# Expert rows on four 64x64 tiles with a folding product, and block attention's small products in four column groups

## What is computed

```python
x = x + attn(layernorm(x))                   # a: heads of 16 features, softmax over features
x = x + mlstm(layernorm(x), ctx, ctx)        # b: gated linear attention on the context
x = x + experts(layernorm(x))                # c: product-key experts + gated MLP
x = x + causal_attention(layernorm(x))       # d
x = x + block_attention(layernorm(x), ctx, mask)  # e: queries pooled over blocks of 16 tokens
x = x + local_layers(x)                      # 6 x (rotary windowed attention, GELU MLP)
```

```python
# c: 4 heads x 8 experts of 4096 for each token, rows of 256 features
scores, indices = top_k of the pairwise sums of two key scores
w = silu(einsum('btd,bthkd->bthk', h, down[indices])) * softmax(scores)
y = einsum('bthk,bthkd->btd', w, up[indices])
y = y + (silu(h @ Wg.T) * (h @ Wu.T)) @ Wd.T
# e: 16 pooled queries a sample, 16 heads of 64, 4 groups of keys
pooled = h.reshape(8, 16, 16, 256).mean(axis=2)
q, k, v = pooled @ Wq, ctx @ Wk, ctx @ Wv      # Wq is 256 x 1024
o = softmax(masked(q k / 8)) v
y = repeat(o @ Wo, 16)                         # Wo is 1024 x 256, each block's row to 16 tokens
```

## Time and profile before

| what | us |
| --- | --- |
| three runs: median (lowest to highest) | 4052.93 (4036.28 to 4060.89) |
| profiled execution | 4046.25 |
| its span in the profile | 4044.5 |
| first product of the local layers | 1091.1 |
| TensorE busy over the span | 3814.3 (94%) |
| mean granted clock of TensorE | 0.972 of full speed |

### The profile page before, as it was taken

One profiled execution on the slowest core, in us unless ns is written; L12 is line 12 of the kernel. 1 busy time (PEld: TensorE's weight loads), 2 busy tenths in 40 slices (PEclk: granted clock), 3 DMA queues, 4 the chain that ended last, 5 costly groups with the idle time before them and its releaser, 6 DMA issues.

```text
span 4044.5 us, 75813 instructions
## 1 busy us (share of the span) xinstructions
PE 3814.3 (94%) x25720; PEld 2763.9 (68%) x25720; DVE 2827.7 (70%) x9152; ACT 2275.8 (56%) x6594; POOL 2242.3 (55%) x2091
## 2 busy tenths in 40 slices
PE   7699999897679999999999999999999999999998
PEld 5577777675346777777777777777777777777766
DVE  4577787775367777777777777777777777777763
ACT  2333443343256666666666666666666666666663
POOL 1555565566266555565565565556555556556540
PEclk8899999999789999999999999999999999999999
DMA  3655555567100001000100001000010000010000
GB/s 118 154 155 144 148 154 141 153 164 201 47 1 6 7 8 35 31 12 6 39 16 27 7 6 37 17 29 4 7 39 14 29 7 27 16 31 14 5 7 27
DMA packets 110543, 210.95 MB, mean 52 GB/s; under 512 B 22321, under 2 KB 71505, under 8 KB 108625
## 3 DMA queue, kind: packets, MB, share of 16 engines
q0 software_dynamic: 40960, 134.25, 12.7%
q1 hardware_dynamic: 69056, 71.71, 5.5%
q10 hardware_dynamic: 144, 0.13, 0.0%
HBM read 191.39 MB, written 2.10 MB: 48 GB/s over the span
## 4 chain that ended last, share of the span: by engine, by line
PE 67%; issue 2%; DVE 2%; POOL 1%; ACT 1%; DMA 0%; SPq 0%; DVEq 0%; POOLq 0%; ACTq 0%
PE pj L1594 23%; PE pj L1674 12%; PE y_ps L1657 8%; PE y_ps L1683 6%; PE sc L1622 5%; PE o_ps L1648 4%; PE tp L1633 4%; PE tp L1602 4%; PE tp L1572 1%; POOL l_qk_rot L1535 1%; ACT l_probs L1753 0%; DVE l_probs L1890 0%; POOL l_r_q L1540 0%; DVE l_qk_cos L1866 0%; POOL l_r_k L1540 0%
## 5 line engine op out<-in xcount | busy, mean ns | idle before, releaser
L1594 PE MATMUL pj<-w_qkv,l_xT 128*128 128x512 f32 x2304 | 1063.1, 598 | 7.2 <-DMA l_qk_gain<-in_gains 3.6
L1535 POOL TENSOR_TENSOR l_qk_rot<-l_qk_cos,l_qk_sin 128x512 f32<-128x512 f32 x384 | 564.8, 1471 | 840.5 <-DVE l_qk_sin L1869 555.7
L382 POOL DMA_INDIRECT f_rows<-in_emb,f_expert x512 | 514.6, 1005 | 382.2 <-PE facc L601 175.0
L1594 PEld LDWEIGHTS pj<-w_qkv,l_xT 128*128 128x128 f32 x2304 | 413.5, 191 | 385.8 <-issue 375.9
L1753 ACT ACTIVATE l_probs<-l_probs,l_low 128x128 f32<-128x128 f32 x1536 | 594.0, 391 | 2.4 <-DVE l_low L1890 0.6
L1674 PE MATMUL pj<-l_xnT,l_w 128*128 128x256 f32 x2112 | 510.9, 387 | 2.2 <-issue 1.2
L1861 DVE TENSOR_REDUCE l_ss<-l_qk_sq 128x8 f32<-128x512 f32 x384 | 261.6, 681 | 324.9 <-ACT l_qk_sq L1740 173.3
L1890 DVE CUSTOM_DVE_ANT_0 l_probs<-sc,l_shut,l_r_q 128x128 f32<-128x128 f32 x1536 | 440.2, 344 | 54.4 <-PE tp L1633 46.7
L1718 ACT ACTIVATE l_qk_raw<-pj 128x512 f32<-128x512 f32 x384 | 227.0, 591 | 434.6 <-PE pj L1594 419.6
L1674 PEld LDWEIGHTS pj<-l_xnT,l_w 128*128 128x128 f32 x2112 | 383.9, 190 | 65.0 <-issue 17.4
L1657 PE MATMUL y_ps<-w_o,l_oT 128*128 128x256 f32 x1536 | 341.2, 380 | 3.5 <-ACT l_oT L1718 3.5
(11 more groups left out here) (324 smaller groups left out, 7164.6 us busy)
## 6 DMA issues: line engine op xcount, KB each, us to landing
w_qkv<-in_L_ffn_Wqkv SPq DMA_DIRECT2D x12, 1024.0 KB
l_w<-in_ff_w SPq DMA_DIRECT2D x6, 1408.0 KB, 6.1
f_rows<-in_emb,f_expert POOLq DMA_INDIRECT x512
w_o<-in_L_ffn_Wo SPq DMA_DIRECT2D x6, 1024.0 KB
w_qkv<-in_L_ffn_Wqkv SPq DMA_DIRECT2D x12, 512.0 KB
l_xf<-l_stream SPq DMA_DIRECT2D x48, 128.0 KB
l_xf<-l_stream SPq DMA_DIRECT2D x48, 127.0 KB
l_w<-in_ff_w SPq DMA_DIRECT2D x6, 768.0 KB, 4.9
```

What stands on the lines that cost most here:

```text
L382: pool.indirect_dma_start(rows[:, j % RH, k, :], None, dram["emb"], bass.IndirectOffsetOnAxis(ap=expert[:, n % 2, at:at + 1], axis=0)).the ...
L1535: pool.tensor_tensor(qk_rot[:, i % ROTS, :], qk_cos[:, b, :], qk_sin[:, b, :], ALU.add).then_inc(rotated if s == 0 else pool_front, 1)
L1594: last = pe.matmul(pj[b][:, :], xT[:, k, t * P:(t + 1) * P], w_qkv[:, k, s * INNER + c * 512:s * INNER + (c + 1) * 512], start=(k == 0), s ...
```

## The change

- `c_up`: a piece's four products of a 128x128 diagonal with 128 rows become eight products of 64x64: tokens 0 to 63 and 64 to 127 are the two row halves, and of two experts the first goes to the same column half and the second to the other one. Row half i adds into a PSUM bank of its own, `acc[i]`. `diag` is 64 columns wide and is made from `pairs`, a 128x64 matrix of two stacked identities.
- `c_y`: each product is split in two column halves, the first for `acc[0]`, the second for `acc[1]`.
- `c_fold` (new): ScalarE copies both banks to SBUF (`folding`, in the space of block attention's scores), and TensorE multiplies each copy with `pairs`, which adds its two halves, into a bank of the ring. `c_add` then reads that bank; `c_copied` takes the place of `c_added`.
- The ring has six banks, since `acc` takes two.
- `e_w` (for `e_w0`, `e_w1`) and `e_y`: the products are spread over four groups of 32 columns, with 16 more operand columns read in each (zeros or neighbours, dropped later); `e_w` is copied by ScalarE alone, `e_q` is two full transposes, and `unpool` is repeated in four groups of 32 partitions and adds the four partial sums of `e_y`.
- GpSimd fills the new constants at the start.
- All five lists of `ORDER` are new. In them `c_fold` comes behind `c_up15` and `c_m5`; `b_cT` and `c_y1` come later in a step than before, and `e_cT` belongs to the step before.

```diff
-    BANKS = 7
+    BANKS = 6
...
-        diag = sb("diag", [P, 2, HALF, P])
+        diag = sb("diag", [P, 2, HALF, HP])
...
-        acc = ctx.enter_context(nc.psum_tensor("facc", [P, TILES, D], F32))
+        acc = [ctx.enter_context(nc.psum_tensor(f"facc{i}", [P, TILES, D], F32)) for i in range(2)]
...
+                fill(pooled[:, KC, :], 0.0)
+                fill(e_o[:, 8 * NB:9 * NB], 0.0)
...
+                fill(pairs[:, :], 0.0)
+                for at in (0, HP):
+                    pool.affine_select(out=pairs[:, :], in_=pairs[:, :], pattern=[[-1, HP]], base=-at, channel_multiplier=1,
+                                       compare_op=ALU.not_equal, fill=1.0).then_inc(set_step, 1)
...
+                for g in range(1, 4):
+                    pool.tensor_copy(unpool[g * QUAD:(g + 1) * QUAD, :], unpool[0:QUAD, :]).then_inc(set_step, 1)
...
             def c_y(half):
                 def down(n):
-                            last = pe.matmul(acc[:, t, :], mT[:, i, t * P:(t + 1) * P], c_wd[:, i, :], ...
+                            for j in range(2):
+                                last = pe.matmul(acc[j][j * HP:(j + 1) * HP, t, :], mT[:, i, t * P + j * HP:t * P + (j + 1) * HP], c_wd[:, i, :], ...
...
             def c_up(j):
-                    for k in range(HALF):
-                        last = pe.matmul(acc[:, j // (HALVES // TILES), :], diag[:, j % 2, k, :], rows[:, j % RH, k, D:2 * D],
+                    for k in range(0, HALF, 2):
+                        for s in range(2):
+                            for i in range(2):
+                                rows_at, out_at = slice(i * HP, (i + 1) * HP), slice((i ^ s) * HP, (i ^ s) * HP + HP)
+                                last = pe.matmul(acc[i][out_at, j // (HALVES // TILES), :], diag[rows_at, j % 2, k + s, :], rows[rows_at, j % RH, k + s, D:2 * D],
...
+            def c_fold(n):
+                pe.wait_ge(c_copied, n + 1)
+                s = Slot("c_fold", n)
+                wait(pe, s.taken, s.before)
+                for i in range(2):
+                    last = pe.matmul(s.bank[i * HP:(i + 1) * HP, :], pairs[:, :], folding[:, i, :, :].rearrange("p t d -> p (t d)"), start=True, stop=True)
+                last.then_inc(ps_full, 1)
...
+            def e_w_(n):
+                for k in range(KC):
+                    for g in range(4):
+                        last = pe.matmul(s.bank[g * QUAD:(g + 1) * QUAD, 0:SEQ], both[:, k * NB:k * NB + QUAD], e_wq[:, k, g * 256:(g + 1) * 256], ...
...
             def e_q(n):
-                for c in range(8):
-                    last = pe.transpose(s.bank[:, c * NB:(c + 1) * NB], e_flat[:, c * P:(c + 1) * P], ident[0:NB, 0:NB])
+                for c in range(2):
+                    last = pe.transpose(s.bank[:, c * P:(c + 1) * P], e_w[:, c * P:(c + 1) * P], ident[:, :])
...
             def e_y_(n):
-                for c in range(8):
-                    last = pe.matmul(s.bank[0:NB, 0:D], e_o[:, c * NB:(c + 1) * NB], e_wo[:, c, :], start=(c == 0), stop=(c == 7))
+                for h in range(2):
+                    for g in range(4):
+                        c = 2 * g + h
+                        last = pe.matmul(s.bank[g * QUAD:(g + 1) * QUAD, 0:D], e_o[:, c * NB:c * NB + QUAD], e_wo[:, c, :], start=(h == 0), stop=(h == 1), ...
...
+            def c_fold(n):
+                act.wait_ge(m_used[0], n + 1)
+                act.wait_ge(m_used[1], n + 1)
+                act.wait_ge(rows_used, HALVES * (n + 1))
+                wait(act, ps_full, Slot("e_pT", n - 1).full if n > 0 else 0)
+                for i in range(2):
+                    last = F(folding[:, i, :, :], acc[i][:, :, :], ACT.Copy)
+                last.then_inc(c_copied, 1)
```

More of the change, by code:

```diff
@@ L55, in first_layers @@
     SCALE = 1.0 / 8.0
+    HP = P // 2
+    QUAD = 32
     ORDER = {}
     ORDER["tensor"] = [
[6 rows of a table removed]
-        ("e_s1", -5), ("c_up7", -4), ("c_up8", -4), ("a_k", -1), ("c_up9", -4), ("e_v", -5), ("e_cT", -4), ("e_pT", -5), ("a_q", -1), ("e_o", -5),
-        ("a_z", -1), ("e_y", -5), ("b_hT", -2), ("c_hT", -3), ("e_u", -5), ("c_q0", -3),
[3 rows of a table added]
+        ("c_up0", -4), ("d_k", -5), ("d_q", -5), ("c_up1", -4), ("d_s", -5), ("d_v", -5), ("a_hT", -1), ("c_up2", -4), ("a_y", -2), ("b_gt", -3),
+        ("d_pT", -5), ("b_m0", -3), ("d_o", -5), ("c_up3", -4), ("b_m1", -3), ("b_qk0", -3), ("b_m2", -3), ("b_qk1", -3), ("b_m3", -3), ("b_qk2", -3),
+        ("b_qk3", -3), ("c_up4", -4), ("b_h0", -3), ("b_h1", -3), ("e_hT", -5), ("c_up5", -4), ("c_up6", -4), ("e_w", -5), ("e_q", -5), ("e_s1", -5),
+        ("a_k", -1), ("e_s0", -5), ("e_v", -5), ("a_q", -1), ("c_up7", -4), ("c_up8", -4), ("c_y1", -4), ("e_pT", -5), ("b_cT", -2), ("e_o", -5),
+        ("a_z", -1), ("c_hT", -3), ("e_y", -5), ("c_up9", -4), ("e_u", -5), ("c_q0", -3),
@@ L78, in first_layers @@
+        ("c_diag4", -4), ("b_m3", -3), ("c_tanh6", -4), ("c_diag5", -4), ("c_diag6", -4), ("e_w", -5), ("e_q", -5), ("c_tanh7", -4), ("c_tanh8", -4),
+        ("c_diag7", -4), ("c_diag8", -4), ("e_v", -5), ("e_exp", -5), ("e_pT", -5), ("a_q", -1), ("c_tanh9", -4), ("b_cT", -2), ("e_o", -5),
+        ("c_diag9", -4), ("e_y", -5), ("c_tanh10", -4), ("c_hT", -3), ("c_diag10", -4),
     ]
     ORDER["vector"] = [
[4 rows of a table removed]
-        ("a_norm", -1), ("d_k", -5), ("b_scan", -3), ("c_m7", -4), ("c_dot3", -4), ("a_y", -2), ("c_coef3", -4), ("d_top", -5), ("b_gt", -3),
@@ L85, in first_layers @@
[L85 to L88, removed]
@@ L141, in first_layers @@
         head_row = sb("head_row", [H4, H4, P])
-        unpool = sb("unpool", [NB, SEQ])
+        unpool = sb("unpool", [P, SEQ])
+        pairs = sb("pairs", [P, HP])
         iota8 = sb("iota8", [P, TOPK])
@@ L662, in e_v_ @@
                 by_token("e_v", n, ctxT_e, e_wv)
-            def e_w(i):
-                def queries(n):
-                    pe.wait_ge(loaded["e"], 16 * LOADS["e"])
-                    pe.wait_ge(e_pooled, n + 1)
-                    s = Slot(f"e_w{i}", n)
-                    wait(pe, s.taken, s.before)
-                    for k in range(KC):
-                        last = pe.matmul(s.bank[0:NB, :], pooled[:, k, :], e_wq[:, k, i * 512:(i + 1) * 512], start=(k == 0), stop=(k == KC - 1))
-                    last.then_inc(ps_full, 1)
-                return queries
+            def e_w_(n):
+                pe.wait_ge(loaded["e"], 16 * LOADS["e"])
+                if n == 0:
+                    pe.wait_ge(consts_set, 2)
+                pe.wait_ge(e_pooled, n + 1)
+                s = Slot("e_w", n)
+                wait(pe, s.taken, s.before)
+                both = pooled[:, :, :].rearrange("p k n -> p (k n)")
+                for k in range(KC):
+                    for g in range(4):
+                        last = pe.matmul(s.bank[g * QUAD:(g + 1) * QUAD, 0:SEQ], both[:, k * NB:k * NB + QUAD], e_wq[:, k, g * 256:(g + 1) * 256],
+                                         start=(k == 0), stop=(k == KC - 1), skip_group_check=True)
+                last.then_inc(ps_full, 1)
             def e_q(n):
-                copied("e_w0", n)
-                copied("e_w1", n)
+                copied("e_w", n)
                 s = Slot("e_q", n)
                 wait(pe, s.taken, s.before)
-                for c in range(8):
-                    last = pe.transpose(s.bank[:, c * NB:(c + 1) * NB], e_flat[:, c * P:(c + 1) * P], ident[0:NB, 0:NB])
+                for c in range(2):
+                    last = pe.transpose(s.bank[:, c * P:(c + 1) * P], e_w[:, c * P:(c + 1) * P], ident[:, :])
                 last.then_inc(ps_full, 1)
@@ L737, in _ @@
             do.update({f"c_up{j}": c_up(j) for j in range(HALVES)})
+            do["c_fold"] = c_fold
             do.update({"a_q": a_q, "a_k": a_k, "a_v": a_v, "a_z": a_z, "a_o": a_o, "a_y": a_y, "b_cT": b_cT, "b_g": b_g, "b_gt": b_gt,
                        "b_h0": b_h0, "b_h1": b_h1, "c_q0": c_q(0), "c_q1": c_q(1), "c_y0": c_y(0), "c_y1": c_y(1),
-                       "d_q": d_q, "d_k": d_k, "d_v": d_v, "d_s": d_s, "d_pT": d_pT_, "d_o": d_o, "e_cT": e_cT, "e_k": e_k, "e_v": e_v_, "e_w0": e_w(0), "e_w1": e_w(1), "e_q": e_q,
+                       "d_q": d_q, "d_k": d_k, "d_v": d_v, "d_s": d_s, "d_pT": d_pT_, "d_o": d_o, "e_cT": e_cT, "e_k": e_k, "e_v": e_v_, "e_w": e_w_, "e_q": e_q,
                        "e_s0": e_s(0), "e_s1": e_s(1), "e_pT": e_pT_, "e_o": e_o_, "e_y": e_y_, "e_u": e_u})
@@ L830, in e_exp, with e_q @@
                 last.then_inc(e_exped, 1)
+            def e_q(n):
+                s = Slot("e_q", n)
+                act.wait_ge(ps_full, s.full)
+                wait(act, ps_full, last_before("e_q", n, "e_s0 e_s1"))
+                F(e_qT[:, :, :].rearrange("p a n -> p (a n)").rearrange("p (g c q) -> p g c q", g=4, c=2),
+                  s.bank[:, 0:2 * P].rearrange("p (c g q) -> p g c q", c=2, g=4)[:, :, :, 0:NB], ACT.Copy).then_inc(s.taken, 1)
```

(4 more changed lines are left out.)

75 lines of the change are left out of this document (41 added, 34 removed), and 34 rows, old and new, of the table ORDER.

## The result

Median 4063.53 us (4039.02 to 4091.7, 20 runs) beside 4053.30 for the kernel before (4036.28 to 4063.0, 20 runs): ratio 1.0033, 95% interval 1.0017 to 1.0050. Forecast were 3974 us, in a range of 3930 to 4015. The profiled execution took 4052.45 us, its span is 4050.7.

What follows compares the result with a forecast made beforehand. TensorE was taken to bound the first part, its work falling from 109.2 to 96.0 us a sample. Gains of 54 (five intervals), 8, 4, 3.5 and 5, less 2.5, make 72: 4046 - 72 = 3974 us, range 3930 to 4015.

Steps and rivals of the forecast that it cites:

- the context's wait: TensorE's wait for the context's DMA ahead of `b_cT`: covered by the new order, -2.1 us idle a sample.
- the last stretch: Last 58 us, sample 7 alone: tiled `e_w` and `e_y` save 6.4, copies and fold add about 3, net 3.5 us.
- the start: GpSimd's eight more small constant instructions ahead of its first power: 2.5 us lost, between 0.8 and 5.8.
- Rival 3: `c_up` tiles adding into one bank don't overlap, 3.4 us a piece for 1.72: 4206 us; chance 0.05.
- the wait at `c_m4`: With six banks, TensorE waits about 2.3 us a sample for the bank of `c_m0`, freed by VectorE after the top-k.
- Rival 4: Copying out of PSUM binds: `c_fold` waits for ScalarE's two copies, 3 us a sample more: 3998 us; chance 0.10.
- Rival 2: VectorE and the six banks become the bound: idle 17, a sample 113 us, 28 us gained: 4018; chance 0.15.
- Idle then is 8.7 - 2.1 + 2.3 + 2.1 = 11.0 and a sample 107.0 us: TensorE's old idle, less DMA wait, plus `c_m4` wait, plus engines waiting on each other; 10.8 us less a sample.
- The two intervals and the first sample: Intervals ending at 930.9 and 1033.1 us, and sample 0 (120 to 233 us): gains of 8, 4 and 5 us.
- the two new handovers ahead of `c_add`: Between last `c_up` and `c_add` in the last stretch: part of about +3 us with copies (0.6 x 2) and fold (1.1).
- The premise: TensorE, busy 93% in the five steady samples, sets the pace at 117.8 us a sample; VectorE not far off.

Runs made afterwards that it cites:

- e16: Changed kernel with half of each `c_up` piece's tiled products left out (8 records for 16): ratio 0.9849.
- e6: Changed kernel, unchanged, rerun and profiled in a plain job (one where the kernel before takes 3994 to 4004 us): 3937.94 us, ratio 0.9834.
- e7: New order with the expert sums of before (128x128 `c_up`, one accumulator, no fold), small products tiled, but six banks for seven: ratio 0.9911.
- e12: The kernel of e4 run again, unchanged, in a job with late TensorE signals: ratio 1.0086.
- e4: Changed kernel with the expert sums of before: 128x128 `c_up`, one accumulator, no fold, seven banks; new order and tiled small products kept: 3959.96 us, ratio 0.9914.
- e1: Kernel before with two of the four products of each `c_up` piece left out, gathers whole: 3962.88 us, ratio 0.9926.
- e15: Repetition of e1, the kernel before with two of four products of each `c_up` piece left out: ratio 0.9966.
- e14: Kernel before with two of four gathers of each piece left out from the second sample on, in a plain job: ratio 0.9852.
- e5: Kernel before, unchanged, rerun and profiled in a plain job: 4003.21 us, ratio 0.9997.
- e3: Changed kernel (tiles, fold, six banks) with the order tables of before, the fold placed behind `c_m7` on TensorE: 4027.64 us, ratio 1.0087.
- e2: Kernel before with a ring of six banks for seven, nothing else: ratio 1.0073.
- e18: Repetition of e14 (kernel before, half the gathers from the second sample on), meant for a late-signal job but run in a plain one: ratio 0.9860.

## Why the prediction was wrong

**What held.** By its own steps: `c_up` 1.02 us a piece (1.13 taken), `e_w` and `e_y` about 1.0 (1.13), `c_y` 3.6 as before, the fold 1.0 (1.1), the context's wait gone, the last stretch shorter by 6.8 us (58.0 to 51.2; 3.5 taken), the start later by 2.3 us (first power at 11.86 for 9.55; 2.5 taken). Rival 3 is out. In a plain job the forecast's numbers hold: a steady sample takes 101.0 us for 113.1, 12.1 less (10.8 taken), TensorE's busy time 94.0 for 108.0 (-14.0; -13.2 taken), idle +1.9 (+2.3 taken), the ratio 0.9834 (0.9805 taken, range 0.970 to 0.991). That is in part luck: the forecast rested on TensorE as the bound, and e16 shows that TensorE doesn't bound the changed kernel; and the idle time there lacks the wait at `c_m4` that its sum has. Rival 4 is out as well, the copies of the fold hide: e6 has no wait of TensorE ahead of the fold, the first profile 2.0 us in five samples. Rival 2's 17 us of idle time is near the 16.0 measured in the first profile, but not by its cause: VectorE is busy 74% there, and six banks cost nothing that shows (e7).

**The steps that failed** are two terms of one sum. The prediction put "Idle then is 8.7 - 2.1 + 2.3 + 2.1 = 11.0 and a sample 107.0 us", with 17 as the upper bound of the idle time, on top of 96.0 us of work. Measured in the first profile: 16.0 us idle a sample (79.9/5), inside its bound, and TensorE's busy time 103.0 where 96.0 were forecast. Together 16.0 + 103.0 = 119.0; of the 12.0 us that are missing, 5.0 are idle time and 7.0 busy time. The 7.0 are a term that the prediction put at nothing without a reason: it priced every record as at before's clock of 0.96, and had no term for a lower clock in the steady samples. The same 3551 records cost 470 us at a clock of 0.96 (e6) and 515 at 0.89. Where TensorE idled more it was granted less, also in e16, so the second is a consequence of the first as far as the rows tell. The two intervals and the first sample, forecast to gain 8, 4 and 5 us, gave -6.9, -0.7 and, with the start, 1.6.

Behind the idle time stand TensorE's late signals. They were in the waits of before in the same five samples, and the prediction doesn't name them:

```profile
POOL f_rows L382 <- remote: 25.0, 10, 2.9
...
DVE x_all L1089 <- remote: 7.4, 5, 1.9
```

It priced the two new handovers ahead of `c_add` at 0.7 us together (about 3 less 1.2 for the copies and 1.1 for the fold). In these jobs TensorE's signal can come 1 to 6 us late wherever gathers run, the fold's 5.4 us late in the sample shown. That this hits an order that hands over tightly harder than one with pieces in between is argued: e12 against e4 shows that the new order with the small products tiled turns from -0.9% to +0.9%, not which of its places does it.

**The premise** that TensorE bounds the sample was half right at most. Taking 13.8 us a sample of its work away (e1, e15) gave 0.3 to 0.7% for 1.7 to 2.2%; taking half the gathers away gave 1.5% (e14). Before is held by both: in the plain job VectorE waits for gathered rows 45.6 us in five samples, and GpSimd 116.1 us for `c_up` to free a row buffer:

```profile
POOL f_rows L382 <- PE facc L601: 116.1, 37, 7.6
...
DVE f_rows L1057 <- DMA f_rows<-in_emb,f_expert: 45.6, 33, 3.4
```

A `c_up` that is shorter and, by the new order, earlier frees the buffer sooner. In e6 that wait is 24.4 us:

```profile
POOL f_rows L400 <- DVE f_expert L1095: 34.3, 5, 7.3
...
POOL f_rows L400 <- PE facc L624: 24.4, 22, 4.0
```

So the saving seems to reach the sample through the gather ring and not only as TensorE's time. It needs the order for that. Over the first part GpSimd waits for `c_up` 173.6 us in e5 and 190.5 in e3, with the tiles in the old order, but 88.6 in e4, in the new order without them, and 50.5 in e6, with both. And the same tiles in the old order gave nothing beyond the six banks (e3 1.0087 beside e2 1.0073, one job), in the new order 0.8%.

**The banks.** The wait of 2.3 us at `c_m4` that I worked out isn't in the waits of the changed kernel, and e7 prices six banks at nothing in the new order. In the old order they cost 29 us (e2). So the sum has a wait in it that isn't there.

**What stays open**: what makes a job one of late signals (the third and the fourth job bore the same number of chip and were of different sorts, so "kind of chip" in the expectations says more than is known); why in such a job a third of ScalarE's and VectorE's raises isn't recorded; whether before loses its 50 us to the same cause, as e18 was to show; and whether it is the new order that loses there, and by which of its places. No version was found that beats both kernels in both sorts: the changed kernel is the best of the complete ones in a plain job, before in the other.

## What to carry to other kernels

A saving on the busiest engine arrives as far as the next ring (here row buffers and gathers) lets it, and the order of the pieces decides how far: price the parts in the order in which they will run, and halve the suspected bound before believing a 93% busy share. Where a sum takes work off TensorE, give it a term for the clock that goes with more idle time. Look for waits put down to `remote` in the trace of before: here they were the mark of signals that came late, and each tight handover that a change adds can pay them again. Run the pair in more than one job before a difference under 2% is called a property of the kernel.

## What the runs showed of the hardware

- TensorE's semaphore raises came 1 to 6 us behind its records (99 of 100 within 6.6 us) in jobs in which the kernel before takes 4046 to 4056 us, 15% of them in before and 25% in the changed kernel; within 0.06 us for 99 of 100 in e5 and e6. Halving the number of gathers brought it to 4%; halving their bytes, with a third fewer packets, left it at 22%.
- Sixteen records of 64x64 tiles that add into two accumulators, 256 columns wide, take 1.02 us from start to start, as the 32 records of 128 columns of the scores; sixteen of 32-column groups the same 1.00.
- The granted clock was lower where TensorE idled more: 0.96 at 7 us idle a sample (e6), 0.89 at 16 (the first profile), and the same records took 45 us more busy time there over five samples.
